# Two moves in a decoder kernel: a pair of roots behind the last tile's affine, and the experts' list product two weight pieces earlier

## The reference, cut to what matters

```python
def _L0_xattn_ref(p, k_v, W_k, b_k, ln_gamma, ln_beta):
    kv = k_v @ W_k.T + b_k
    out = jnp.einsum('bij,bjd->bid', p, kv)
    sim = jnp.einsum('bid,bjd->bij', out, kv) * scale
    mu = jnp.mean(sim, axis=-1, keepdims=True)
    var = jnp.var(sim, axis=-1, keepdims=True)
    sim = (sim - mu) * jax.lax.rsqrt(var + EPS) * ln_gamma + ln_beta
    return jax.nn.softmax(sim, axis=-1)
...
x = _layernorm(x + _L0_xattn_ref(x, ctx_512, ...), axis=-1)
x = _layernorm(x + _L0_ffn_ref(x, ...), axis=-1)
```

## Time and profile before

| | us |
|---|---|
| median of 3 runs | 1415.07 |
| the 3 runs | 1415.07, 1415.04, 1422.34 |
| profiled execution | 1407.76 |
| its span, first to last instruction | 1405.8 |
| PE busy | 1272.7 (91%) |
| DVE busy | 813.6 (58%) |
| ACT busy | 548.4 (39%) |
| POOL busy | 523.1 (37%) |
| the cross attention's block, from the end of the barrier | about 260.3 to 304.1 |
| the experts' block | about 304.1 to 461.9 |

### The profile page before, as it was taken

One profiled execution on the slowest core, in us unless ns is written; L12 is line 12 of the kernel. 1 busy time (PEld: TensorE's weight loads), 2 busy tenths in 40 slices (PEclk: granted clock), 3 DMA queues, 4 the chain that ended last, 5 costly groups with the idle time before them and its releaser, 6 DMA issues. The chain is left out here.

```text
span 1405.8 us, 25099 instructions
## 1 busy us (share of the span) xinstructions
PE 1272.7 (91%) x9172; PEld 842.6 (60%) x9172; DVE 813.6 (58%) x1826; ACT 548.4 (39%) x1273; POOL 523.1 (37%) x597
## 2 busy tenths in 40 slices
PE   7999999847896877999999977799999989999998
PEld 4868778635555444677777766345555555344487
DVE  5464655556354475676776423577777773743343
ACT  4554636233223576767667331144344351000010
POOL 3452627530751367476577301322222201500010
PEclk9999999958898798999999977899999999999999
DMA  3010038533886201212122120100000206542100
GB/s 132 24 37 15 22 108 277 202 125 148 237 251 200 79 11 24 43 31 40 34 38 26 20 43 1 62 20 21 21 22 30 63 1 172 180 139 68 34 8 23
DMA packets 144168, 106.57 MB, mean 76 GB/s; under 512 B 87873, under 2 KB 130089, under 8 KB 142913
## 3 DMA queue, kind: packets, MB, share of 16 engines
q1 hardware_dynamic: 135904, 88.31, 22.0%
q0 software_dynamic: 4496, 13.33, 3.6%
q10 hardware_dynamic: 3664, 3.55, 0.8%
HBM read 84.16 MB, written 22.35 MB: 76 GB/s over the span
## 5 line engine op out<-in xcount | busy, mean ns | idle before, releaser
L2811 PE MATMUL la_banks<-la_xe,la_f_w 128*128 128x512 f32 x348 | 151.4, 593 | 3.5 <-DVE la_xe L3189 3.5
L2170 DVE SCALAR_TENSOR_TENSOR dh_front<-dh_pj,df_conv,dh_front 128x510 f32<-128x510 f32 x144 | 107.4, 746 | 76.2 <-ACT dh_front L1909 72.4
L3352 POOL TENSOR_TENSOR la_area<-la_area 128x512 f32<-128x512 f32 x48 | 60.3, 1277 | 172.4 <-DVE la_area L3032 152.0
L2811 PEld LDWEIGHTS la_banks<-la_xe,la_f_w 128*128 128x128 f32 x348 | 65.4, 190 | 83.6 <-issue 83.6
L346 POOL TENSOR_TENSOR wa_qkT<-lf_area 128x512 f32<-128x512 f32 x40 | 50.7, 1268 | 96.8 <-DVE lf_area L318 96.8
L3189 DVE TENSOR_TENSOR la_xe<-xT,la_area 128x1024 f32<-128x1024 f32 x29 | 52.6, 1830 | 55.5 <-PE la_banks L2811 48.1
L2929 ACT ACTIVATE la_area<-la_banks,la_nmax 128x256 f32<-128x256 f32 x128 | 59.0, 475 | 58.5 <-DVE la_nmax L3041 58.5
L350 POOL TENSOR_TENSOR mw_gu<-mw_gu,const 128x384 f32<-128x384 f32 x64 | 63.6, 999 | 30.0 <-ACT mw_gu L381 30.0
L3372 POOL TENSOR_TENSOR la_o_rstd<-la_o_var,la_minus_half 128x1 f32<-128x1 f32 x8 | 6.4, 803 | 164.3 <-DVE la_o_var L3251 164.3
L2937 ACT COPY la_area<-la_banks 128x512 f32<-128x512 f32 x64 | 37.5, 590 | 56.2 <-PE la_banks L2660 55.9
L273 PE MATMUL wa_po<-wa_wo,mw_rows 128*128 128x256 f32 x256 | 56.6, 379 | 0.0
(11 more groups left out here) (621 smaller groups left out, 3090.1 us busy)
## 6 DMA issues: line engine op xcount, KB each, us to landing
mw_gu<-in_L_ffn_gate_up SPq DMA_DIRECT2D x16, 768.0 KB, 14.2
placed<-mw_rows SPq DMA_DIRECT2D x8, 768.0 KB, 10.7
mw_d<-in_L_ffn_down SPq DMA_DIRECT2D x16, 384.0 KB, 13.6
mw_rows<-placed SPq DMA_DIRECT2D x8, 768.0 KB, 6.8
la_area<-w_table POOLq DMA_DIRECT2D x6, 1024.0 KB, 12.2
pairs<-me_picked SPq DMA_DIRECT2D x7, 704.0 KB, 3.9
la_f_w<-in_L_ffn_q_proj SPq DMA_DIRECT2D x32, 128.0 KB, 2.2
la_f_w<-in_L_ffn_k_proj SPq DMA_DIRECT2D x32, 128.0 KB, 2.4
```

Source lines behind the costliest of these rows:

```text
L2170: dve.scalar_tensor_tensor(dst, src[:, :, 0:SEQ - j], conv[:, a, m, D_CONV - 1 - j:D_CONV - j], dst, ALU.mult, ALU.add).then_inc(tapped, 1)
L2811: mm = pe.matmul(acc[c][m], f_w[n % SLOTS][:, m, k, :], xe[(n - U) % RING][:, k, :], start=first and k == 0, stop=last and k == KC - 1)
L3352: pool.tensor_tensor(qrot[:, c, n, :], prod[:, c, 2 * n, :], prod[:, c, 2 * n + 1, :], ALU.add).then_inc(rotated, 1)
```

## The change

One piece moves in each block, and nothing is added or removed.

- POOL in `cross_with_norms`: `root(2, 0)` is issued behind the affine of tile 7, directly ahead of `root(2, 1)`.
- PE in `routed_experts`: the list product, with its wait for the lists, stands behind `absorb(2)` in place of `absorb(4)`. The two transpositions of the merged lists, with their wait, stand behind `absorb(3)`.

```diff
                     pool.tensor_tensor(n3[:, t % RING, :], n2[:, t % RING, :], be_sb[:], ALU.add).then_inc(shifted, 1)
-                    if t == TILES - 2:
-                        root(2, 0)
+                root(2, 0)
                 root(2, 1)
...
-                for n in range(1, OTHERS - 2):
+                for n in range(1, 3):
                     absorb(n)
                 pe.wait_ge(half_listed, 1)
                 pe.matmul(op[0:M_E, 1, 2 * M_E:2 * M_E + M_CAP], env.c("ident")[M_E:P, M_E:P], lists[M_E:P, :], start=True, stop=True).then_inc(brought, 1)
+                absorb(3)
                 pe.wait_ge(listed, 2)
                 pe.transpose(op[:, 1, 0:M_E], heads[:].rearrange("e j s -> e (j s)"), env.c("ident")[0:M_E, 0:M_E])
                 pe.transpose(op[:, 1, M_E:2 * M_E], tails[:].rearrange("e j s -> e (j s)"), env.c("ident")[0:M_E, 0:M_E]).then_inc(lists_turned, 1)
-                for n in range(OTHERS - 2, OTHERS):
+                for n in range(4, OTHERS):
                     absorb(n)
```

## The result

| | before | changed | ratio, 95% interval |
|---|---|---|---|
| median of 22 runs each, us | 1417.59 | 1412.50 | 0.9963 (0.9950 to 0.9976) |
| profiled execution, us | 1407.76 | 1416.23 | |

The change takes 5.1 us off the median. The forecast was 4.8 (1410.3 in absolute time, from the 1415.07 of before's first three runs), and a time within 0.5% of before had the highest chance. Two of before's 22 runs took 1693.42 and 2549.20 us and are left out of the ratio; the median of the other 20 is 1417.01, so that the difference is between 4.5 and 5.1 us.

What follows compares the result with a forecast made beforehand. It took the cross attention's tile 7 chain, then lists and gathers early and DMA work late in the experts' block, as bounds. −2.6 − 2.2 = −4.8 us gave a median of 1410.3 us, range 1404.5 to 1416.5.

Steps and rivals of the forecast that it cites:

- The root, −2.6 us: Cross attention, tile 7: the affine no longer waits for the root, so DVE and the chain to the barrier come 2.6 us earlier.
- The rival that it does nothing: Cross attention: DVE's own order holds tile 7, so the root's move is worth nothing, 1412.9 us; chance 2 in 100.
- The start of the lists' chain, 4.4 to 4.9 us earlier: Experts' block: the earlier list product lets transpositions and gathers start 4.4 to 4.9 us earlier, with a new 1.4 us PE wait.
- The loads the other way: Experts' block: weight loads of groups 4 and 5 go out 1.8 and 3.2 us later, groups 6 and 7 3.2 earlier.
- The block's end, −2.2 us: Experts' block: DMA work bounds the end; closing a hole in it, less the later start, gains 2.2 us, bounds 0 to 4.9.
- The gathers' pace to the end: Experts' block: the end comes as much earlier as the gathers start, −7.5 us in all, 1407.6; chance 0.20.
- The loads that give it all back: Experts' block: the later load start eats the hole, leaving only −2.6 us, 1412.5; chance 0.18 including a root that fails.
- The clock rival: Experts' block: PE's clock stays at half for three more groups, +7.0 us, 1422.1; chance 0.07 including anything that disturbs a run.
- the prediction's sign for this rival: Experts' block: PE's granted clock under 0.70 between the list product and 378 would show that the clock made it slower.
- PE's second wait for gathers: Experts' block: PE's two waits for gathers were to stay about as long as before, 2.95 and 2.74 us.
- The last `hidden_of`: Experts' block: a sign that the forecast is right, to come 2 us earlier within the block.

Runs made afterwards that it cites:

- the stores' wait put off: Only the root moved, plus DVE's wait for the weight pieces' stores moved from weights step 0 to step 2, against the kernel before: 1403.27 us, ratio 0.9988.
- the change again: The changed kernel run and profiled once more, against the kernel before in the same rounds: 1402.73 us against 1405.46, ratio 0.9970.
- light loads: Groups 8 to 15 load half their gate and up weights; against the kernel before, 0.9940 with only the root moved, 0.9929 with the whole change.
- the root alone: Only the root's move in the cross attention, experts' block unchanged, against the kernel before: 1402.08 us against 1405.46, ratio 0.9973.
- The lists alone: Only the list product and transpositions moved, the root as before, against the kernel before: 1404.83 us against 1405.46, ratio 0.9988.
- the change with the wait put off: The changed kernel with DVE's wait for the weight pieces' stores moved from weights step 0 to step 2, against the kernel before: 1402.39 us, ratio 0.9975.
- the two orders: List product behind absorb(2), as changed, or behind absorb(3) with transpositions behind absorb(4), root moved; the latter against the kernel before: 0.9953, then 0.9970.
- the change with light loads and the wait put off: The change with halved gate and up loads for groups 8 to 15 and DVE's stores wait two groups later, against the kernel before: 1409.09 us, 0.9937.

## Why the prediction was right

**The root, −2.6 us.** Right in every step. The affine follows at once, DVE's moments are what limits the gain, the root's 1.02 us are covered, and the way to the next block is 2.7 us shorter in all twelve profiles with the move. Timed alone it is 3.8 (2.2 to 5.3), and 1.7 (0.1 to 3.4) with the stores' wait put off. The rival that it does nothing is excluded.

**The start of the lists' chain, 4.4 to 4.9 us earlier.** Right, and a little more: 5.0 in the recorded profile, with waits of 1.29 and 1.02 us for the 1.4 and 1.0 of the text, and 4.10 for merging. Later profiles with the same move have 5.0 to 6.0.

**The loads the other way.** Right in sign and size in the recorded profile: +1.7 for the expected +1.8, +3.1 for +3.2, −3.5 for −3.2. In that of the change again, where PE ran at the lower clock, it is +0.7, +4.6 and +0.8.

**The block's end, −2.2 us.** The mechanism, the DMA engines' work, is what the runs on the faster chips speak for: light loads take 4.6 us off the root alone, and in their profiles the early gathers last to the end. The size was on the high side. The lists alone are worth 1.7 us (0 to 3.4). Beside the root they are worth 0.4 in the first set (0.9970 to 0.9973), 1.8 in the second (0.9975 to 0.9988) and 1.5 with light loads. The step that seems too generous took the same 0.95 to 1.00 of the DMA engines for the stretch up to SP's first tails as for the whole, and the gain there as the gain at the end. SP is past the first tails at least 4.5 us earlier, more than the 0.6 to 3.7 of the text (in which 31.8 us at 0.95 are 33.5 and not 33.4, which changes nothing), and what the engines have not done by then is paid behind it, in a stretch that is 2 to 8 us longer. The sum came out all the same: the main interval is 3.4 to 7.1 us, the forecast 4.8. That 5.1 lies so near is in part luck, since the change again gave 4.2 and the change with the wait put off 3.5. And for the recorded runs the second half's path isn't shown: in their profile the late activation holds the block up, and the DMA share behind the first tails is 0.90 and not 0.98.

**The rivals.** The gathers' pace to the end (−7.5) is excluded by the main interval and by all the others of the change. The loads that give it all back (−2.6) lie outside the main interval, and inside those of the change again (2.4 to 6.0) and of the change with the wait put off (1.7 to 5.2). So the truth is likely between the forecast and this rival. The clock rival has its event and not its price. In the profile of the change again the granted clock does fall behind the new waits, and from 344 to 354 PE runs at the lower level:

```profile
344.00:354.00 10.00, 10.00 (x40) 8.34 (x41) 1.76 (x7) 2.60 (x6) 6.35 (x7) 0.50 0.79 268
```

In the profile of the recorded run it doesn't, though its waits at the same two places are no shorter (1.29 and 1.02 us, against 0.47 and 1.03 in the change again):

```profile
338.70:348.00 9.30, 8.28 (x60) 6.38 (x58) 4.38 (x21) 4.52 (x13) 3.32 (x3) 1.00 0.68 238
```

From the product to 378 the granted clock is 0.79 in the recorded profile and 0.78 in the change again, so the prediction's sign for this rival, under 0.70, is absent. The Trainium skill ("TensorE: Matmul & The Clock Gate", Part 1) says that the number of slow matmuls at a kernel's start differs from run to run of the same kernel; the two rows, from the middle of this kernel, agree that it can. The lost clock has no price that shows: the execution with it has its last `hidden_of` at 108.5, against 109.5 and 111.6 in the other two profiles with full loads and the same lists.

**The signs.** Of the signs that the prediction named, no idle of POOL ahead of the last affine, the earlier scaling, PE's new wait, the earlier gather and the closed hole are all there. PE's second wait for gathers was to stay near 2.7 us and is 0.46; it is 0.22 and 1.18 with the root alone too, so this isn't the lists' doing. The last `hidden_of` was to come 2 us earlier in the block. It comes 4.7 us earlier in the change again and 1.6 in the change with the wait put off, but also 1.8 and 2.6 earlier with the root alone, so single profiles can't carry this sign.

**What the prediction missed.** DVE's wait for the stores, which the code holds in plain sight behind a loop index, and ACT's late activation. Putting the first off didn't change the time. What the second does to the change's gain isn't known.

## What to carry to other kernels

When an edit starts a chain earlier, count two things at the place where the bound changes: what arrives earlier there, and what work is then still queued. A chain that gains 5 us ahead of a saturated stretch keeps, by the account here, only the part by which a hole in the transfers is closed. Look also for every wait in the engines' lists that was satisfied by being late: such a wait has no row in the profile of before.

A third point is for the placing of a product among filler work, and the runs suggest it rather than prove it. Put it behind the piece in which its input gets ready, and not before: the wait of 1.3 us that this saves is small, but every piece behind it, and the load that hangs on that piece, comes later by it. Here the two orders differ by some 2 us, within their errors.

## What the runs showed that I had not expected

ACT's late activation came in two of the fourteen profiles, those of the change as recorded and of the change with light loads and the wait put off, both times beside a kernel before of 1417.6 to 1417.7 us and not 1405 to 1406. It is the same to 0.03 us: 9.97 and 15.91, and 10.00 and 15.90. In both it ends as the last gathers' traffic ends (DMA share 0.58, 0.20 and 0.00 in the two-microsecond windows from 374, 376 and 378 of the recorded run). The trace names the releaser only as remote. The Trainium skill ("Runtime: NRT & Kernel Launch", "Instruction fetch mechanics") says that engines fetch their instructions in blocks by DMA while they run; a late block could look like this. But in the rows of the instruction queues of the recorded run no block moves between 360 and 382, so none lands when ACT goes on, and this wasn't shown.

The kernel before has no profile beside those slower runs, so whether it has the wait there too stays open. The sizes speak for it. The experts' block is 14.7 us longer in the recorded profile than in that of the change again (166.5 against 151.8), and 15.9 longer with light loads (162.8 against 146.9). The medians of these two kernels are 9.8 and 14.2 us higher there, and that of the kernel before is 12 higher. So the late activation is probably most of what makes those runs slower, for before and changed alike. This would also explain how SP's load behind the first tails can be 9.7 us later in the block than in the profile of before, while the median is 5.1 us better than before's.

The other surprise is that difference itself: the kernel before takes 1405 to 1406 us beside most of the experiments and 1417.6 to 1417.7 beside two of the measurements. That is more than twice the effect that was to be explained, so only ratios within one set of runs could be used.
